# Transformer layer on eight cores: the second half's normalisation is interleaved with the down projection, and two weight loads are issued earlier

## What is computed

```python
# --- layer 0 (seq_preln) ---
x = x + _L0_attn_ref(_layernorm(x), Wq, Wk, Wv, Wo, q_gamma, k_gamma)   # adds its own input, too
x = x + _L0_ffn_ref(_layernorm(x), gate_w, up_w, down_w, gate_scale, up_scale, down_scale)

def _quantized_matmul(x, w, scale):      # weights rounded to float8_e4m3
    return einsum('bsi,io->bso', x, w.astype(float8_e4m3fn).astype(x.dtype)) * scale
def _L0_ffn_ref(x, ...):                 # gate, up: 2048 x 6144; down: 6144 x 2048
    gate = silu(_quantized_matmul(x, gate_w, gate_scale))
    up = _quantized_matmul(x, up_w, up_scale)
    return _quantized_matmul(gate * up, down_w, down_scale)
```

## Time and profile before

| what | us |
|---|---|
| timed runs, two | 6251.29 and 6641.9, median 6446.59 |
| the profiled execution, its own time | 6269.65 |
| its span on the slowest core (core 0) | 6267.8 |
| spans of the eight cores | 6210.8 to 6267.8 |
| core 0, gate and up step of half 0 | 4106.3 to 4771 |
| core 0, down step of half 0 | 4772.1 to 5188 |
| core 0, gate and up step of half 1 | 5188.5 to 5852 |
| core 0, down step of half 1 | 5853.1 to 6262 |

### The profile page before, as it was taken

One profiled execution on the slowest core, in us unless ns is written; L12 is line 12 of the kernel. 1 busy time (PEld: TensorE's weight loads), 2 busy tenths in 40 slices (PEclk: granted clock), 3 DMA queues, 4 the chain that ended last, 5 costly groups with the idle time before them and its releaser, 6 DMA issues.

```text
span 6267.8 us, 56797 instructions; the slowest of 8 cores (6210.8 to 6267.8 us)
## 1 busy us (share of the span) xinstructions
PE 4519.5 (72%) x16213; PEld 1588.8 (25%) x16536; DVE 1671.0 (27%) x3095; ACT 1698.0 (27%) x2511; POOL 293.9 (5%) x231
## 2 busy tenths in 40 slices
PE   4555546665666656666567667479997999999998
PEld 1111111111111211111111111134443434444433
DVE  2433324433333333333333333321113001111000
ACT  3232323312444145553155556000110000101000
POOL 0000000000000100000000000100000010000000
PEclk9666556576776867788678888789998999999987
DMA  4111021144110711102510100955656986655895
GB/s 88 54 32 50 27 47 21 21 67 59 16 21 1 113 15 14 21 1 41 80 14 7 21 1 1 116 68 35 41 40 83 83 75 50 41 38 37 61 73 58
DMA packets 670617, 271.20 MB, mean 43 GB/s; under 512 B 541286, under 2 KB 611942, under 8 KB 670318
## 3 DMA queue, kind: packets, MB, share of 16 engines
q0 software_dynamic: 598576, 147.86, 31.3%
q1 hardware_dynamic: 71742, 119.68, 7.3%
HBM read 532.77 MB, written 33.57 MB: 90 GB/s over the span
## 4 chain that ended last, share of the span: by engine, by line
PE 52%; ACT 16%; DVE 13%; issue 7%; DMA 6%; another core or an unknown queue 4%; DVEq 1%; ACTq 1%; SPq 0%; POOL 0%; POOLq 0%
PE ps L112 39%; PE lacc L112 13%; ACT pbt L124 8%; DMA wofc<-wo 4%; ACT xnn L124 3%; ACT rowb L124 3%; DVE pbt L132 2%; DVE xnn L132 2%; DVE rowb L132 2%; DVE xtmp L132 1%; ACT rlrow L124 1%; DMA x1f<-x1s 1%; DVE rlB L132 1%; DVE outt L132 1%
## 5 line engine op out<-in xcount | busy, mean ns | idle before, releaser
L124 ACT ACTIVATE pbt<-ps,biasB,rall 128x512 bf16<-128x512 f32 x1280 | 994.6, 777 | 790.3 <-PE ps L112 411.1
L112 PE MATMUL ps<-pbt,vtok 128*128 128x512 bf16 x1234 | 574.9, 466 | 438.3 <-DVE pbt L132 235.2
L112 PE MATMUL lacc<-fuse,dbuf 128*128 128x512 bf16 x3011 | 721.1, 402 | 107.3 <-DVE outt L132 100.8
L112 PE MATMUL ps<-xn,gbuf 128*128 128x512 bf16 x3010 | 691.3, 380 | 90.1 <-DVE xn L132 86.8
L112 PE MATMUL ps<-xn,ubuf 128*128 128x512 bf16 x3010 | 689.8, 379 | 3.2
L112 PE MATMUL ps<-qhat,khat 128*128 128x512 bf16 x1259 | 598.8, 480 | 24.3 <-DVE pbt L132 12.2
L124 ACT ACTIVATE gact<-ps,gs_sb 128x512 bf16<-128x512 f32 x192 | 131.9, 687 | 1604.5 <-PE ps L112 1561.0
L132 DVE SCALAR_TENSOR_TENSOR fuse<-ps,us_sb,gact 128x512 bf16<-128x512 f32 x192 | 144.1, 750 | 1183.8 <-PE ps L112 1134.2
L112 PEld LDWEIGHTS lacc<-fuse,dbuf 128*128 128x128 fp8e4 x3072 | 311.9, 102 | 516.7 <-issue 265.6
L132 DVE TENSOR_TENSOR pbt<-pbt 128x512 bf16<-128x512 bf16 x640 | 272.1, 425 | 543.8 <-ACT pbt L124 516.5
L112 PEld LDWEIGHTS ps<-xn,gbuf 128*128 128x128 fp8e4 x3072 | 300.7, 98 | 450.8 <-issue 89.2
(11 more groups left out here) (97 smaller groups left out, 2761.4 us busy)
## 6 DMA issues: line engine op xcount, KB each, us to landing
xtt<-xT SPq DMA_DIRECT2D x128, 256.0 KB, 3.3
wqhg<-wq POOLq DMA_DIRECT2D x32, 1024.0 KB, 9.2
wofc<-wo POOLq DMA_DIRECT2D x64, 512.0 KB, 9.6
gbuf<-gw POOLq DMA_DIRECT2D x48, 512.0 KB, 9.9
ubuf<-uw POOLq DMA_DIRECT2D x48, 512.0 KB, 14.1
dbuf<-dw POOLq DMA_DIRECT2D x32, 768.0 KB, 17.6
xtt<-xq SPq DMA_DIRECT2D x64, 256.0 KB, 7.5
x1s<-x1t SPq DMA_DIRECT2D x64, 256.0 KB, 6.2
```

The costliest lines, as they stand in the source:

```text
L112: eng.matmul(o, l, r, start=st, stop=sp))
L124: eng.activation(out=o, in_=i, func=f, **kw).then_inc(sem["S"], 1))
```

## The change

Three things change in the FFN part, all in the order of instructions; what is computed stays.

1. `xn2_prep` no longer appends its instructions at once but returns 34 closures: for each `tc2` one for the two row loads and 16 for the tiles. Half 0's all run at once, as before. Half 1's run three at a time behind each block of half 0's down step, so they are spread over the first 12 blocks.
2. TensorE's wait for all of `xn2` ahead of every group becomes a wait for the tile of its own `tc2`, in the first two groups of a half only.
3. The first two down weight loads of a half are issued with chunks 22 and 23, behind their gate and up weights; so `dbuf` 0 now stands ahead of chunk 23's weights on GpSimd's list. The later ones are issued behind the block that frees their buffer, which is the same place in GpSimd's list as before.

```diff
             def xn2_prep(hf):
+                va = {0: {}, 1: {}}
+                i2d = {}
+                cls = []
                 for tc2 in range(2):
...
+                    cls.append(mk_i2())
                     for fc in range(FC):
...
+                                va[tc2][fc] = v_a
+                                if fc == FC - 1:
+                                    gd[f"inv2B{tc2}"] = ("V", v_a)
+                            return fn
+                        cls.append(mk_tile())
+                return cls, va
+
+            cls0, va0 = xn2_prep(0)
+            for fn in cls0:
+                fn()
+            cls1, va1 = xn2_prep(1)
+            dwd_h = {}
             for hf in range(2):
+                va = va0 if hf == 0 else va1
+                if hf == 1:
+                    while cls1:
+                        cls1.pop(0)()
...
+                    if ich in (ICH - 2, ICH - 1):
+                        pre = ich - (ICH - 2)
+                        gwait("gpsimd", gd.get(f"dbuf{pre}"))
+                        dwd_h[pre] = dma(
+                            "gpsimd", dbuf[pre].bitcast(FP8)[:, :],
+                            dw[:, pre * 128:(pre + 1) * 128]
+                            .rearrange("(icg p) f -> p icg f", p=128), f"DW{pre}")
...
                             wait("tensor", f"GU{wbuf}", gud)
-                            wait("tensor", "V", v_xn2)
                             gwait("tensor", gd.get(f"gub{alt % 2}"))
+                            if ich == 0 and icsub == 0:
+                                wait("tensor", "V", va[tc2][FC - 1])
...
                 gd["xn2w"] = ("T", cnt["T"])
-                if hf == 0:
-                    v_xn2_next = xn2_prep(1)
...
-                    gwait("gpsimd", gd.get(f"dbuf{wbuf}"))
-                    dwd = dma("gpsimd", dbuf[wbuf].bitcast(FP8)[:, :],
-                              dw[:, fc * 128:(fc + 1) * 128].rearrange("(icg p) f -> p icg f", p=128),
-                              f"DW{wbuf}")
+                    dwd = dwd_h[fc]
...
                     gd[f"dbuf{wbuf}"] = ("T", t_dn)
+                    if fc + 2 < FC:
+                        gwait("gpsimd", gd.get(f"dbuf{wbuf}"))
+                        dwd_h[fc + 2] = dma(
+                            "gpsimd", dbuf[wbuf].bitcast(FP8)[:, :],
+                            dw[:, (fc + 2) * 128:(fc + 3) * 128]
+                            .rearrange("(icg p) f -> p icg f", p=128), f"DW{wbuf}")
...
-                if hf == 0:
-                    v_xn2 = v_xn2_next
+                    if hf == 0:
+                        for _ in range(3):
+                            if cls1:
+                                cls1.pop(0)()
```

More of the change, by code:

```diff
@@ L944, in xn2_prep @@
-                    for fc in range(FC):
[L945 to L957, removed]
@@ L958, in xn2_prep, with mk_i2, fn @@
-                    gd[f"inv2B{tc2}"] = ("V", cnt["V"])
-                return cnt["V"]
-            v_xn2 = xn2_prep(0)
+                    def mk_i2(tc2=tc2, qc=qc):
+                        def fn():
+                            gwait("sync", gd.get(f"inv2B{tc2}"))
+                            dma("sync", inv2B[tc2][:, :],
+                                rbc[inv2_slot[qc]:inv2_slot[qc] + 1, :]
+                                .broadcast_to([128, 512]), f"I2{tc2}")
+                            i2d[tc2] = dma(
+                                "sync", minv2B[tc2][:, :],
+                                rbc[minv2_slot[qc]:minv2_slot[qc] + 1, :]
+                                .broadcast_to([128, 512]), f"I2{tc2}")
+                        return fn
@@ new lines, in xn2_prep, with mk_tile, fn @@
+                    cls.append(mk_i2())
+                    for fc in range(FC):
+                        def mk_tile(tc2=tc2, qc=qc, fc=fc):
+                            def fn():
+                                sl4 = (tc2 * FC + fc) % 4
+                                gwait("sync", gd.get(f"x1f{sl4}"))
+                                xfd = dma("sync", x1f[sl4][:, :],
+                                          x1s[fc, :, qc * 512:(qc + 1) * 512], f"XF{sl4}")
+                                wait("vector", f"XF{sl4}", xfd)
+                                wait("vector", f"I2{tc2}", i2d[tc2])
+                                gwait("vector", gd.get("xn2w"))
+                                vop("tensor_tensor", fft[:, :], x1f[sl4][:, :],
+                                    inv2B[tc2][:, :], ALU.mult)
+                                v_a = vop("tensor_tensor",
+                                          xn2[:, fc * 1024 + tc2 * 512:
+                                              fc * 1024 + (tc2 + 1) * 512],
+                                          fft[:, :], minv2B[tc2][:, :], ALU.subtract,
+                                          inc=True)
+                                gd[f"x1f{sl4}"] = ("V", v_a)
+                                va[tc2][fc] = v_a
+                                if fc == FC - 1:
+                                    gd[f"inv2B{tc2}"] = ("V", v_a)
+                            return fn
+                        cls.append(mk_tile())
@@ L1008, in _build @@
                     gd[f"gbuf{wbuf}"] = ("T", cnt["T"])
-                v_fuse = cnt["V"]
+                    v_fuse = cnt["V"]
                 gd["xn2w"] = ("T", cnt["T"])
-                if hf == 0:
-                    v_xn2_next = xn2_prep(1)
                 DB = [PS_L0, PS_L1]
```

## The result

| | runs compared | their median, us | ratio to before, 95% interval |
|---|---|---|---|
| before | 5 of 10 | 6256.7 | |
| changed | 6 of 11 | 6219.6 (6206.35 to 6232.16) | 0.9942 (0.9926 to 0.9958) |

Both kernels also have executions some per cent longer, in which cores of a die show a lower granted clock (the 6641.9 of the first pair is one); all comparisons here leave them out. The change takes 6256.7 x 0.0058 = 36 us off, with an interval of 26 to 46. The forecast was 6215 us and 45.2 us of gain, and "within 2%". The direction was right, and 45.2 lies just inside the interval, 9 us above its middle. Wrong was the statement that so small a gain cannot be told from none: the interval is 0.16% to either side, and 0.58% lies clear of it. Wrong was also to let the middle of the first two runs, 6446.59, set the upper end of the range.

A forecast was written before the change was run, and what follows sets the result against it. TensorE bounds gate and up; the down steps lose time to waiting and lower clock. 38.3 + 6.9 = 45.2 us off 6269.65 gives 6224.5, off 6251.29 gives 6206.1; forecast the middle, 6215 us, range 6185 to 6405.

The forecast's parts named there:

- The 38.3 us: Half 0's down step: spreading half 1's preparation cuts the 40.34 us wait before block 1 to 2.06, gaining 38.3 us.
- The 6.9 us: Start of the FFN part: 32 matmuls move into the old pause, 8.39 us less 1.47 for a second pause.
- my 1.47: Start of half 0: the first group after the second pause takes 4.93 us to the next instead of 3.46.
- 0 for change 3: Issuing a half's first down loads earlier gains nothing and costs 0, with an upper bound of 21 us for both halves.
- The rival of chunk 23: Chunk 23's weights come late in both halves, costing up to 21 us, likely about 12: 6236 us; chance 0.12.
- The price of a tile load, 0.57 us: Half 0's down step: each x1f load delays down weights 0.57 us, three 1.7; upper bound 1.38 each, 4.1 for three.
- the cost of 0 for late down weights: Half 0's down step: core 0's weights land in 18.7 us, under 24.4, costing 0; core 6 waits about 10 us.
- The share of 1.58: Busy share in the old preparation's burst in half 0's down step, taken to say that packets of two queues overlap.
- The rival of the clock: Half 0's down step on core 0 or 2 runs like core 0's slow second, adding 32.2 us: 6256.7; chance 0.14.
- The rival of transfers: Down steps become bound by weight loads; core 6 loses 101 us in eleven blocks: 6310 us, slower than before; chance 0.04.
- The resolution: Whole kernel: a measurement can tell about 2%, 125 us, from no change, so the forecast gain counts as the same.
- The signs: Profile marks named beforehand for right (375 to 382 us down step) or wrong (dbuf waits, span moved over 60 us).

The follow-up runs named there:

- e15: The changed kernel with two instead of three preparation pieces behind each block, the last two of 34 at half 1's start; ratio to before 0.9939.
- e7: The changed kernel with odd down-step blocks using the two PSUM banks that the FFN part leaves unused; ratio to before 0.9862.
- e8: e7 with a third buffer for down weights, room made by multiplying in place in x1f; 6115.4 us, ratio to before 0.9779.
- e1: The changed kernel with only change 1 kept: full wait for xn2 and down loads where they were; ratio to before 0.9958.
- e4: Changes 1 and 2 without change 3, against before; ratio to before 0.9948.
- e9: The changed kernel without the 32 x1f tile loads of half 1; median of six runs 6207.4 us, ratio to before 0.9922.
- e10: The changed kernel with a third buffer for down weights, tile loads kept; median of five runs 6202.6 us, ratio to before 0.9913.
- e14: The changed kernel run again unedited, beside the third-buffer kernel on one chip; 6206.3 us, ratio to before 0.9908.

## Why the prediction was right and wrong

**The 38.3 us** of the wait before block 1: right. The waits for `outt` on core 0 fell from 100.8 to 62.8 us, by 38.0.

**The 6.9 us** of the split wait: right. The stretch from the first wait to the first down matmul is 4.8 to 7.6 us shorter in the mean over the cores. The matmuls behind the second pause again ran slower: the first gate group there takes 6.03 us to the next on core 0 (4113.28 to 4119.31) where 3.45 is usual, and 4.81 to 6.03 over the cores. So the second pause costs 1.4 to 2.6 us, 2.1 in the mean, for my 1.47. The rule of the Trainium skill, page "TensorE: Matmul & The Clock Gate", section "Part 1: The HAM clock gate", that the array is slow unless recent activity released it, agrees with this.

**0 for change 3**: right within what can be told. The rival of chunk 23 came true on single cores: before the chunk's first matmul core 4 waited 3.6 us for `ubuf` here, and one core each waited 2.3 us in e15, 0.4 in e7 and 3.7 in e8. No core did in before, e1 or e4, where the down loads stand behind chunk 23's weights. So change 3 costs a little now and then, and no run shows that it gains anything.

**The price of a tile load, 0.57 us,** is the step of the sum that failed, and with it the cost of 0 for late down weights on all cores but core 6. I took the lower bound from one down load in the old burst, and counted 13 more transfers beside it. Of the 15 `x1f` loads only 11 were issued between that down load (4793.6) and its landing (4818.0), from 4795.5 to 4817.5, one by one as VectorE freed the buffers. Counted so, there were 7 more than the four of a block, and the price would have been 7.4 / 7 = 1.06. And two single landings, 24.4 and 17.0, are a weak base on a core whose 16 landings in half 0 spread like this (core 0, before):

```profile
DMA to landing us min/median/max: 15.0/17.1/31.7
```

In the changed kernel, with the loads issued just behind the down load of each block, three lengthened the landing by 3.0 to 3.3 us (22.4 against 19.1 before and 19.4 in e9). By the rule of the Trainium skill ("DMA: Bandwidth & Descriptors", section "Queues, rings and completion order") it would have been 4.1; the measured 3.0 to 3.3 is nearer to it than my 1.7. The share of 1.58 did not speak against that rule as I had read it. The share also exceeds 1 where only GpSimd's queue moves data, so it doesn't show that packets of two queues overlap. The queues of core 0 of before, 4720 to 4741 us (packets, MB, share of 16 engines):

```profile
q0 software_dynamic: 6212, 1.30, 117.9%
q8 instruction: 1, 0.02, 0.3%
```

That the count matters in proportion isn't shown: e15 with two in a block had 22.2. From this price followed that core 0 pays nothing and only core 6 about 10 us. In fact core 6 waited 0, 3.8 and 2.7 us in the three profiles of the changed kernel, and core 0 0, 2.6 and 13.7. The waits fall on any core: 0 to 12 us in one profile, 0 to 16 in the next, up to 31 in e4, in the mean 3.5 to 6.0. A core's median landing in one execution did not tell which core has the least room in the next.

With the measured waits in place of that term, the FFN times close within 2.3 us, on the base of 2208.6: 45.2 less 3.5, 5.0 and 4.5 gives 41.7, 40.2 and 40.7 for the three profiles of the changed kernel, where 44.0, 40.0 and 39.7 were measured. 38.3 less 3.5 gives 34.8 for e1 (35.3), 45.2 less 6.0 gives 39.2 for e4 (39.3), and 45.2 stands for e10 (47.5).

**The timed gain** then was 36 us (26 to 46) and in e14 58 (39 to 76); 45.2 lies between. Whether 9 us were missing at all in the first comparison is open, and so is what the waits of 3.5 to 5.0 us in the mean cost the slowest core. What the mean core gains, 40 to 44 us, fits both.

**The rival of the clock**: did not happen. No down step in the three profiles of the changed kernel took the 409 us of core 0's second; the longest was 393.8, with 15.9 us of waits for weights. And it was not needed to explain the gain: the timed runs of before lie at 6249 to 6261, not at the profile's 6269.65. I had forecast from the middle, 6260, and their median is 6256.7; that one run and one profile had this for their middle was luck in part.

**The rival of transfers** was the right mechanism, far below its price: it had 101 us on core 6, and the waits for weights were 16 us at most in the three profiles of the changed kernel and 31.3 in e4. It sets the time on all cores only when the slack of a block goes (e7).

**The resolution**, "about 2%" and 125 us, is the other step that failed: it made a gain of 45.2 us count as none. It was taken over without a reason from the rows. The five runs of before in the comparison spread by 12 us, 0.2%, which two runs could not show, and the change of 0.58% was measured to 0.16%.

**The signs** that I had named. Of those for wrong, waits for `dbuf` in half 0's down step came on cores 1, 2 and 4, a wait ahead of chunk 23 on core 4, and core 0's span moved by 67 us, of which 29 lie in its second down step (408.9 to 380.0). Of those for right, the down weights should have landed in 18 to 19 us on core 0 and took 20.6; and the first gate group started 27 to 30 us before the second pair, not 34. Half 0's down step of 375 to 382 us came on six cores; cores 1 and 4, which waited for weights, took 383.8 and 386.2. Its clock was 0.96 on core 6 and 0.97 on core 0.

## What to carry to other kernels

A block of work written in one piece between two dependent steps of an in-order engine costs the other engine its whole length; give it out in pieces sized to what the step leaves free, and let none be left for the moment when the consumer needs the last. When an engine's waits go, look at what its inputs have as slack: here two weight buffers were nearly enough for a block of 22.9 us (3.5 to 5.0 us of waits) and not for one of 20.7 (22.0), and a third buffer with a second pair of banks took off another 81 to 102 us. And add up waits per core before comparing slowest cores: the mean over cores closed to 2.3 us where timed runs scattered by 10 and more.

## What was not expected of the hardware

The pauses of 2.06 us in every block also went with a lower clock. With two pairs of banks and three buffers TensorE ran the down steps at 1.00 instead of 0.96. From the start of half 0's down step to that of half 1's it is 996.1 us (310.6 + 685.5, core 1) instead of 1041.5 (376.8 + 664.7, core 0 of the changed kernel). Of these 45.4 us, 31 are pauses and the other 14 slower matmuls: each of the 15 pauses of 2 us cost about 3.

The landing of a down load and TensorE's waiting for it went separate ways: 25.6 us in e8 with 0.5 us of waiting for `dbuf` in the mean, 22.4 in the changed kernel with 3.0.
